# Expert phase in pairs of tiles, and products without a reader in the pause ahead of it

## The reference, cut to what matters

```
x = x + xattn(layernorm(x), ctx, ctx, Wq, Wk, Wv, Wo, bo, mask)
n = layernorm(x).reshape(8192, 256)
logits = n @ router_w.T + router_b                 # 32 experts
routed = argmax(logits)                            # one expert for each token
y_all[e] = relu(relu(n @ w1[e] + b1[e]) @ w2[e] + b2[e])    # 256 -> 64 -> 256
x = x + y_all[routed, token]
```

## Time and profile before

| what | value |
|---|---|
| median of 3 runs | 1811.64 us |
| profiled execution, its own time | 1811.58 us |
| span of that execution | 1809.8 us |
| PE busy | 1753.6 us (97%) |
| DVE busy | 1247.4 us (69%) |
| ACT busy | 1033.9 us (57%) |
| POOL busy | 282.4 us (16%) |

### The profile page before, as it was taken

How to read it: one execution, slowest core, us unless ns; L and a number is a source line. 1 busy time by engine, 2 the same in 40 slices (tenths; PEclk the granted TensorE clock), 3 DMA queues, 4 the chain that set the end, 5 groups by cost and what they waited for, 6 DMA issues and landing times. The chain is left out here.

```text
span 1809.8 us, 42548 instructions
## 1 busy us (share of the span) xinstructions
PE 1753.6 (97%) x12580; PEld 1356.3 (75%) x12581; DVE 1247.4 (69%) x5361; ACT 1033.9 (57%) x3206; POOL 282.4 (16%) x377
## 2 busy tenths in 40 slices
PE   5999999999999999999999999999999996899997
PEld 4777788778877887777877788788778874566664
DVE  5677777777777777777777777777777776233332
ACT  4656666666666666666666666666666663343442
POOL 1011011111111111111111111111101111233333
PEclk9999999999999999999999999999999998555555
DMA  7830000000000000000000000000000000333321
GB/s 209 237 99 21 24 24 24 22 21 24 24 24 24 24 24 24 24 24 24 20 22 24 24 24 24 24 24 24 24 24 18 18 12 16 90 101 101 86 70 24
DMA packets 70009, 77.61 MB, mean 43 GB/s; under 512 B 11703, under 2 KB 64093, under 8 KB 69985
## 3 DMA queue, kind: packets, MB, share of 16 engines
q1 hardware_dynamic: 61778, 60.18, 11.9%
q0 software_dynamic: 7680, 16.93, 2.6%
q10 hardware_dynamic: 528, 0.22, 0.0%
HBM read 47.60 MB, written 33.88 MB: 45 GB/s over the span
## 5 line engine op out<-in xcount | busy, mean ns | idle before, releaser
L672 ACT ACTIVATE Sm<-Sm,mneg 128x128 f32<-128x128 f32 (+1 forms) x1024 | 455.5, 448 | 366.9 <-DVE mneg L904 366.1
L904 DVE CUSTOM_DVE_ANT_0 Sm<-psS,MK 128x128 f32<-128x128 f32 (+1 forms) x1024 | 304.4, 353 | 123.7 <-PE psS L519 114.0
L546 PE MATMUL psO<-PT,V 128*64 128x256 f32 x2048 | 277.5, 392 | 2.3 <-ACT PT L665 2.0
L519 PE MATMUL psS<-KT,QT 64*128 64x128 f32 (+1 forms) x2048 | 238.5, 351 | 4.4 <-DVE mneg L904 2.6
L530 PEld LDWEIGHTS psT<-ident,Sm 128*128 128x128 f32 x1536 | 163.7, 141 | 98.7 <-issue 98.1
L530 PE MATMUL psT<-ident,Sm 128*128 128x128 f32 x1536 | 224.6, 282 | 0.0
L546 PEld LDWEIGHTS psO<-PT,V 128*64 128x64 f32 x2048 | 124.3, 136 | 123.8 <-issue 74.6
L665 ACT ACTIVATE PT<-psT 128x768 f32<-128x768 f32 x256 | 205.5, 803 | 6.6 <-PE psT L530 2.5
L672 ACT ACTIVATION_READ_ACCUMULATOR Sm<-Sm,mneg 128x1 f32 x1024 | 195.1, 191 | 0.0
L921 DVE TENSOR_TENSOR Sm<-Sm,rinv 128x512 f32<-128x512 f32 x256 | 192.8, 753 | 0.0
L519 PEld LDWEIGHTS psS<-KT,QT 64*128 64x128 f32 x2048 | 134.9, 187 | 59.7 <-issue 44.3
(11 more groups left out here) (151 smaller groups left out, 3229.8 us busy)
## 6 DMA issues: line engine op xcount, KB each, us to landing
lists<-pad SPq DMA_DIRECT2D x8, 1560.0 KB, 16.4
XS<-lists SPq DMA_DIRECT2D x96, 130.0 KB, 2.1
x_in<-in_x SPq DMA_DIRECT2D x32, 256.0 KB, 2.7
ctx_in<-in_ctx SPq DMA_DIRECT2D x32, 256.0 KB, 2.7
xr<-in_x SPq DMA_DIRECT2D x32, 256.0 KB, 2.7
W2R<-in_L_ffn_weights SPq DMA_DIRECT2D x1, 2048.0 KB
out<-Y,tok POOLq DMA_INDIRECT x96, 2.6
W2R<-in_L_xattn_Wq SPq DMA_DIRECT2D x1, 1024.0 KB, 10.1
```

Source lines behind the costliest of these rows:

```text
L519: last = nc.tensor.matmul(psS[:, side, o:o + (it + 1) * P], QT[rows, p, it * P:(it + 1) * P], KT[rows, p, 0:(it + 1) * P], start=True, sto ...
L546: last = nc.tensor.matmul(psO[DH * side:DH * side + DH, 0:N], V[:, t, DH * h:DH * h + DH], PT[:, side, cols], start=(t == 0), stop=(t == 1))
L672: nc.scalar.activation(v, v, ACT.Exp, bias=mneg[:, p % 2, k:k + 1], scale=-1.0, accum_out=rsum[:, p % 2, k:k + 1]).then_inc(s_exp, 1)
L904: nc.vector.tensor_tensor_reduce(out=Sm[:, p % 4, side, cols], in0=psS[:, side, cols], in1=MK[:, cols], scale=-SCALE, scalar=3e38, op0=ALU ...
```

## The change

The tile buffers become pair buffers: each of the eight holds two tiles that follow each other. The number of tiles stays 96, in 48 pairs (`NP`). In the expert phase:

- One load brings 256 rows, 260 KB. It waits for `s_y` (the buffer's last use by DVE) and no more for the DMA that wrote the rows out.
- DVE normalises the two tiles one after the other, adds relu and residual for both in one instruction of 512 columns, and now copies w1 of the second tile of each pair, for which it reads the expert number too. ACT copies w1 of the first.
- PE does four transposes, four products with w1 (the second tile's go to PSUM rows 64 to 127, and the two tiles alternate), and two products with w2. ACT copies both transposed tiles with one instruction of 512 columns, and does two bias-and-relu instructions of 128 columns, reading two expert numbers for them. The bias comes from a table `B1T` that holds b1 transposed in both halves of the partitions, so b1 is no more part of `W1`.
- POOL issues two indirect DMAs for each pair, one behind the other.

Around it: b1 is loaded twice (one small DMA more at the start); 34 products of 512 columns, whose results are not read, stand at the end of PE's program of the first part; 3 float32 products of 512 columns, not read either, stand in the second part between the transpose of `owner` and the wait for `tile_row`. The ones in `HT` are set by DVE after `tile_row` instead of ahead of it.

```diff
-    NET = -(-(NT + E - 1) // U) * U
+    NP = B * N // P // 2 + E // 2
+    NET = 2 * NP
...
             ranks(B - 1)
+
+            for _ in range(34):
+                nc.tensor.matmul(psR[0][:, :], Woh[:, 0:1, 0:P].rearrange("p a d -> p (a d)"),
+                                 Wh["q"][:, 0:1, 0:512].rearrange("p a n -> p (a n)"), start=True, stop=True)
...
-            act.dma_start(b1_in[:], b1).then_inc(s_small, 16)
+            for half in range(2):
+                act.dma_start(b1_in[:, half, :], b1).then_inc(s_small, 16)
...
-            nc.vector.memset(W1R[HID:P, :, KD * HID], 0.0)
-            nc.vector.tensor_copy(W1R[0:HID, :, KD * HID], psS[0:HID, 1, 0:E]).then_inc(s_b1r, 1)
+            nc.vector.tensor_copy(B1T[:], psS[:, 1, 0:E]).then_inc(s_b1r, 1)
...
+                with pool.Fori(0, NP // U) as i:
                     for u in range(U):
                         wait_apart(pool, s_passed, s_y, U * i + u + 1)
-                        nc.gpsimd.indirect_dma_start(out_rows, bass.IndirectOffsetOnAxis(ap=tok[u][:], axis=0),
-                                                     Y[u][:], None, bounds_check=last_token, oob_is_err=False
-                                                     ).then_inc(s_done[u], 16)
+                        for t in range(2):
+                            nc.gpsimd.indirect_dma_start(out_rows, bass.IndirectOffsetOnAxis(ap=tok[u][:, t:t + 1], axis=0),
+                                                         Y[u][:, t, :], None, bounds_check=last_token, oob_is_err=False
+                                                         ).then_inc(s_done[u], 16)
...
-                    sp.dma_start(XS[u][:], lists[bass.ds((U * i + u) * P, P), :]).then_inc(s_in[u], 16)
+                    sp.dma_start(XS[u][:], lists[bass.ds((U * i + u) * 2 * P, 2 * P), :].rearrange("(t p) r -> p t r", p=P)
+                                 ).then_inc(s_in[u], 16)
...
-                        wait_apart(sp, s_passed, s_done[u], 16 * i)
+                        wait_apart(sp, s_passed, s_y, U * (i - 1) + u + 1)
...
+                def norm_pair(i, u):
                     dve.wait_ge(s_in[u], 16 * i + 16)
+                    for t in range(2):
+                        last = nc.vector.tensor_scalar(XH[u][:, t, :], XS[u][:, t, 0:D], XS[u][:, t, D:D + 1],
+                                                       XS[u][:, t, D + 1:D + 2], ALU.subtract, ALU.mult)
+                    last.then_inc(s_xh, 1)
+
+                def add_pair(i, u, free):
+
+                    if free:
+                        wait_apart(dve, s_passed, s_done[u], 32 * i)
+                    nc.vector.tensor_copy(tok[u][:], XS[u][:, :, D + 2])
                     dve.wait_ge(s_y_pe, U * i + u + 1)
+                    nc.vector.scalar_tensor_tensor(out=Y[u][:], in0=psY[u % 2][:, :, 0:D], scalar=0.0,
+                                                   in1=XS[u][:, :, 0:D], op0=ALU.max, op1=ALU.add).then_inc(s_y, 1)
+
+                def w1_copy(i, u):
+                    e = expert(dve, U * i + u, 1)
+                    nc.vector.tensor_copy(W1[u][:, 1, :], W1R[:, bass.ds(e, 1), :].rearrange("p a c -> p (a c)")
+                                          ).then_inc(s_w1[1], 1)
...
                 def hidden(i, u):
+                    e = [expert(act, U * i + u, t) for t in range(2)]
                     act.wait_ge(s_h_pe, U * i + u + 1)
+                    for t in range(2):
+                        last = nc.scalar.activation(HT[u][0:HID, t, :], psH[u % 2][half(t), 0:P], ACT.Relu,
+                                                    bias=B1T[half(t), bass.ds(e[t], 1)])
+                    last.then_inc(s_h, 1)
...
                 nc.tensor.transpose(psR[1][0:1, 0:P], owner[:], ident[:]).then_inc(s_te_pe, 1)
+                pe.wait_ge(s_w1r, 16)
+                for _ in range(3):
+                    nc.tensor.matmul(psR[0][:, :], ident[:], W1R[:, 0:4, 0:P], start=True, stop=True)
                 pe.wait_ge(s_row, 1)
...
                     for c in range(KD):
+                        for t in range(2):
+                            last = nc.tensor.matmul(psH[u % 2][half(t), 0:P], W1[u][:, t, c * HID:(c + 1) * HID], XHT[u][:, t, c, :],
+                                                    start=(c == 0), stop=(c == KD - 1))
                     last.then_inc(s_h_pe, 1)
...
                 def y_of(i, u, free=True):
+                    e = [expert(pe, U * i + u, t) for t in range(2)]
                     if free:
                         pe.wait_ge(s_y, U * i + u - 1)
+                    pe.wait_ge(s_h, U * i + u + 1)
+                    for t in range(2):
+                        last = nc.tensor.matmul(psY[u % 2][:, t, 0:D], HT[u][:, t, :],
+                                                W2R[0:HID + 1, bass.ds(e[t], 1), :].rearrange("p a d -> p (a d)"),
+                                                start=True, stop=True)
+                    last.then_inc(s_y_pe, 1)
```

More of the change, by code:

```diff
@@ L413, in _ @@
             root1(1)
-            pool.wait_ge(s_small, 64)
+            pool.wait_ge(s_small, 80)
             iteration(0, False, True)
@@ L1016, in attention_moe @@
         tile_row = kept("tile_row", [1, P], I32)
[L1017 to L1023, removed]
+        XS = [kept(f"XS{u}", [P, 2, ROW]) for u in range(U)]
+        XH = [kept(f"XH{u}", [P, 2, D]) for u in range(U)]
+        W1 = [kept(f"W1_{u}", [P, 2, KD * HID]) for u in range(U)]
+        XHT = [kept(f"XHT{u}", [P, 2, KD, P]) for u in range(U)]
+        HT = [kept(f"HT{u}", [HID + 1, 2, P]) for u in range(U)]
+        Y = [kept(f"Y{u}", [P, 2, D]) for u in range(U)]
+        tok = [kept(f"tok{u}", [P, 2], I32) for u in range(U)]
         s_ht1 = sem("ht_ones")
@@ L1029, in attention_moe @@
         s_in = [sem(f"tile_in{u}") for u in range(U)]
-        s_w1 = sem("w1_copied")
+        s_w1 = [sem(f"w1_copied{t}") for t in range(2)]
         s_xh = sem("xh_ready")
@@ L1038, in attention_moe, with expert, half @@
         s_done = [sem(f"tile_out{u}") for u in range(U)]
-        psXT = [psS[:, u, :] for u in range(2)]
-        psH = [psT[:, u, :] for u in range(2)]
-        psY = [psO, psW]
+        psXT = [psO, psW]
+        psH = psR
+        psY = [psS, psT]
         out_rows = out.rearrange("b n d -> (b n) d")
+        def expert(eng, j, t):
+            return eng.value_load(tile_row[0:1, bass.ds(2 * j + t, 1)], min_val=0, max_val=E - 1)
+        def half(t):
+            return slice(HID * t, HID * t + HID)
         with nc.Block() as block2:
@@ L1065, in load @@
                 def load(i, u):
[L1066 removed]
+                    sp.dma_start(XS[u][:], lists[bass.ds((U * i + u) * 2 * P, 2 * P), :].rearrange("(t p) r -> p t r", p=P)
+                                 ).then_inc(s_in[u], 16)
                 for u in range(U):
                     load(0, u)
[L1070 removed]
+                with sp.Fori(1, NP // U) as i:
                     for u in range(U):
[L1073 removed]
+                        wait_apart(sp, s_passed, s_y, U * (i - 1) + u + 1)
                         load(i, u)
                 for u in range(U):
[L1076 removed]
+                    sp.wait_ge(s_done[u], 32 * (NP // U))
             @block2.vector
             def _(dve):
[L1080 to L1082 removed]
                 dve.wait_ge(s_te_pe, 1)
@@ new lines, in w1_copy @@
+                def w1_copy(i, u):
+                    e = expert(dve, U * i + u, 1)
+                    nc.vector.tensor_copy(W1[u][:, 1, :], W1R[:, bass.ds(e, 1), :].rearrange("p a c -> p (a c)")
+                                          ).then_inc(s_w1[1], 1)
+                AHEAD = 3
+                for u in range(U):
+                    last = nc.vector.memset(HT[u][HID:HID + 1, :, :], 1.0)
+                last.then_inc(s_ht1, 1)
+                dve.wait_ge(s_row, 1)
+                dve.wait_ge(s_w1r, 16)
@@ L1139, in _, with pairs_of @@
                     xht(0, u)
-                def tiles_of(i, more):
+                def pairs_of(i, more):
                     for u in range(U):
@@ L1163, in turn @@
                         pe.wait_ge(s_xht, U * i + u - 1)
-                    xh = XH[u][:].rearrange("p (d c) -> p c d", c=KD)
-                    for c in range(KD):
-                        last = nc.tensor.transpose(psXT[u % 2][:, c * P:(c + 1) * P], xh[:, c, :], ident[:])
+                    for t in range(2):
+                        xh = XH[u][:, t, :].rearrange("p (d c) -> p c d", c=KD)
+                        for c in range(KD):
+                            o = (t * KD + c) * P
+                            last = nc.tensor.transpose(psXT[u % 2][:, o:o + P], xh[:, c, :], ident[:])
                     last.then_inc(s_xh_pe, 1)
@@ L1191, in _, with pairs_of @@
                 hid(0, 0, False)
-                def tiles_of(i, first, more):
+                def pairs_of(i, first, more):
                     for u in range(U):
```

78 lines of the change are left out of this document (35 added, 43 removed).

## The result

The changed kernel takes **1746.6 us** (median of 4 runs, 1746.1 to 1747.0), the kernel before 1811.9 beside it: a ratio of 0.964, 95% interval 0.9623 to 0.9657. The forecast was 1695, with a range of 1682 to 1740. The change is faster by 65 us where 116 were forecast, and the time lies outside the range.

The account below looks back on a forecast made before the run. PE at half clock was taken to bound the expert phase, 2.625 us a tile. With POOL bounding instead: first scatter 1554, 129.3 to the 48th pair, last scatter ending 1685.7, drain 8.1, plus 1.8, gives 1695 us; range 1682 to 1740.

Parts of the forecast that it names:

- all waits between the engines reach back a pair: Expert phase: every wait between PE, ACT and DVE reaches back at least a pair; their sums lie below POOL's 2.75 us.
- at 1.00 to the end: TensorE's clock line: full clock from about 1536 us through the whole expert phase.
- rival A: Expert phase: clock stays low or falls back, PE bounds at 4.2 us a pair, about 1765 us; chance 0.15.
- rival B: Expert phase: chain of waits through the engines, or POOL at its dearest, 3.0 to 3.6 a pair, 1707 to 1736; chance 0.15.
- Once lost it does not come back: Argument for rival A: PE busy without a break for 84 us at 0.50 did not raise the clock.
- The 34 products: End of PE's first part: 8.0 us at full clock, 16.0 at half; the fill costs nothing, at worst 4 us.
- The start: Start of expert phase: first turn about 1548.0 instead of 1546.84, +1.2 us, bounds 0 and +4; first scatter 1554.
- POOL the bound at 2.75 a pair: Expert phase: two scatters a pair, 2 x (1.076 + 0.30) = 2.75 us, the longest engine sum; forecast chance 0.66.
- PE's 2.1: PE's work per pair at full clock: transposes 0.47, hid 0.6, y 1.02, sum 2.1 us, bounds 2.0 and 2.5.
- Rival C: POOL's scatters starve beside DVE: from 2.33 us each no gain, at 2.4 gives 1817; chance 0.03 with Rival D.
- Rival D: Clock low and hid's eight MATMULs taking turns: 5.26 us a pair, about 1816; chance 0.03 with Rival C.
- Transfers: DMA engines: 1.8 us a pair, under 2.75; the loads' new wait for DVE eight pairs back costs nothing.

Follow-up runs that it names:

- e18: The changed kernel, unedited, run on chip 8: 1744.4 us, ratio 0.9634.
- e9: The changed kernel with the load of XS waiting for the landing of the pair's scatters instead of DVE's add, chip 4: 1689.0 us, ratio 0.9322.
- e15: e9 unedited, run on chip 11: 1745.6 us over five runs, ratio 0.9634.
- e1: The changed kernel without its 34 and 3 unread products, chip 11: 1745.5 us, ratio 0.9634.
- e2: The changed kernel with one more unread 512-column float32 product ahead of the transposes of each of the first eight pairs, chip 11: 1748.2 us, ratio 0.9649.
- e3: The changed kernel with one more unread 256-column float32 product ahead of the transposes of every pair, chip 11: 1734.4 us, ratio 0.957.
- e14: e9 without the 34 and the 3 products, chip 3: five runs, 1688.5, 1690.0, 1690.9, 1715.9 and 1734.6 us.
- e16: e14 unedited, run on chip 11: 1745.7 us over five runs, ratio 0.9639.
- e12: The changed kernel with the load of XS waiting for DVE's add of the pair after the next one, chip 3: 1688.0 us, ratio 0.9317.
- e13: The changed kernel with the load of XS waiting for DVE's add one pair later, chip 3: 1688.8 us, ratio 0.9321.
- e7: The changed kernel with one scatter a pair, the second tile of each pair not written, chip 10: 1672.9 us, ratio 0.9236.
- e17: The changed kernel with the load of XS waiting for DVE's next normalisation instead of its add, chip 11: 1745.7 us, ratio 0.9638.
- e4: The kernel before (single tiles) with only the 34 and 3 products added, chip 11: four runs, 1796.9, 1744.2, 1795.3 and 1776.9 us.

## Why the prediction was wrong, point by point

- **The failed step** is that all waits between the engines reach back a pair and so cost nothing, and with it the clock "at 1.00 to the end". In the traces of the changed kernel and of e18 the reports of PE come up to 3.1 us late from the third pair on, PE idles, and the clock falls at about 1563. This is rival A, at 0.15, entered through rival B's standstills. The cost: about 43 pairs at 3.92 in place of 2.75, 43 x 1.17 = 50 us, and 1695 + 50 + 2 for the start is the measured 1747. Against e9's 2.585 a pair it is 43 x 1.335 = 57 us, the distance from e9 to e15.
- **Rival A's price** was 4.2 a pair and 1765; 3.92 was measured. Turn was put at 1.12 and takes 0.99, y at 2.04 and takes 1.87; hid at 1.05 was right. 0.28 x 48 = 13 us, most of the 18 between.
- **"Once lost it does not come back"** (said of rival A) holds for the changed kernel, e1 and e2: PE busy 84 of 84 us, clock 0.50. It does not hold in e3, which regains it several times.
- **Prompt reports alone are no guarantee.** On chip 3, where none was late, e14 lost the clock in two of its five runs, in the profiled one behind a slow register read. The forecast had no term for that.
- **The 34 products**: their own step was right. They end near 1542.3, ahead of POOL's drain, and the barrier opens at 1544.8 (1544.0 said). That they carry the clock through the phase was wrong where it mattered: e1, and e15 against e16, show no value. On chip 3, e14 without them lost the clock in two runs of five, and e12 and e13 with them in none of four; that is too few to tell.
- **The start**: first turn 1548.93 (1548.0 said), first scatter 1555.8 (1554 said), together 1 to 2 us.
- **POOL the bound at 2.75 a pair**: shown right in kind by e9 on chip 4, with 2.585. The mis-sized term is the scatter beside a busy DVE, 0.974 us and not 1.076; the 0.30 of issue was exact. 0.165 x 47 = 8 us less, 1.5 later at the start: 1689 for 1695. (0.974 is the middle one in e9; the mean is 0.985.)
- **PE's 2.1**: PE's busy time in e7 is 73.12 / 80 x 2.39 = 2.18 a pair.
- **Rival C** is refuted: a scatter takes 975 ns in the mean over the changed kernel's 96, and 985 in e9 beside a DVE busy 39.72 of 60 us, against the 2.33 from which it would decide. Its own sums were a little off: at 9.6 us for each 0.1, 2.4 us a scatter gives 1823 and not 1817, and the time before is reached from 2.28. The Trainium skill, SBUF — State Buffer, "A bandwidth-pool intuition that's wrong", would have had an estimated 4.9 us by its ratio of five; the trace doesn't agree with that ratio for these scatters, the longest of which took 1.135 us (e9).
- **Rival D** is refuted by hid's 1.06 for eight MATMULs.
- **Transfers**: the new wait of the loads costs nothing, as said, as far as chips can be compared: 1745.7 with e17's wait and 1745.6 with e15's on chip 11, 1688.0 and 1688.8 for two others on chip 3.
- **The drain** after the last scatter (1735.22 + 0.98 = 1736.2) is 8.1 us, as said.

## What to carry to other kernels

When a gain hangs on the clock, look for the waits that leave PE without input when one of them takes 1 or 2 us longer, and price the phase at both clocks. The chance of the good case is then the chance that the hand-offs are prompt times the chance that the clock holds, and it is smaller than either. An experiment that looks like a cure needs the uncured kernel beside it on the same chip: here nine of the ten kernels on chips 10, 4 and 3 seemed to cure a fault that their chips did not have. Where "nothing was busy" is all that the rows say of a wait, the times of the semaphore increments tell whether the sender or the receiver was late. Dummy products are worth trying where the work that follows doesn't raise the clock by itself (e4), not where it does (e1).

## What was not expected of the hardware

- One kernel took 1689.0 us on chip 4 and 1745.6 on chip 11, with all of the difference in the last 200 us, while the kernel before took 1811.9 and 1811.1 there.
- PE's reports came up to 4.5 us after the end of their product (a hid in e15, reported at 1562.4), in traces that also lack 16 to 28% of part one's completions. Whether the chip delays the reports, or the recording of them does, is open: every run here was recorded.
- The clock fell after a stretch with PE busy 6.93 of 10 us (e2), held for the 80 us of e7's window at 9.1 of 10 and for the 60 of e9's at 8.7, and came back in e3.
- On a chip where no report was late, reads of an expert number on PE, ACT and DVE took 578 to 737 ns at the same moment (about 300 in the middle), and the clock fell 2 us after the gap (e14).
